# A two-layer transformer stack on one core: the second layer's first weight split is moved into the first layer's last steps

## The reference

```python
x = x + _layernorm(_L0_attn_ref(_layernorm(x), Wq, Wk, Wv, Wo))            # 32 heads, 8 key heads, rotary, causal
x = x + _layernorm(_L0_ffn_ref(_layernorm(x), lora_A, lora_B, W, bias, lora_weights))   # one 512x512 linear with LoRA
x = x + _layernorm(_L1_attn_ref(_layernorm(x), Wq, bq, Wk, bk, Wv, bv, Wo, bo, gq, gk)) # 32 heads, below
x = x + _layernorm(_L1_ffn_ref(_layernorm(x), w1, w3, w2, ...))                         # gated, 1376 wide

def _L1_attn_ref(hidden_states, Wq, bq, Wk, bk, Wv, bv, Wo, bo, gq, gk):
    q = rmsnorm((hidden_states @ Wq + bq).reshape(b, n, 32, 128), gq)
    k = rmsnorm((hidden_states @ Wk + bk).reshape(b, n, 32, 128), gk)
    v = (hidden_states @ Wv + bv).reshape(b, n, 32, 128)
    attn = softmax(einsum('bnhd,bmhd->bhnm', q, k) / sqrt(128))
    return einsum('bhnm,bmhd->bnhd', attn, v).reshape(b, n, 4096) @ Wo + bo
```

## Time and profile before

| | us |
|---|---|
| median of 3 runs | 2296.71 |
| profiled execution, its own time | 2295.63 |
| span of the profiled execution | 2293.8 |
| PE busy | 2107.2 (92%) |
| DVE busy | 1666.9 (73%) |
| ACT busy | 1350.7 (59%) |
| POOL busy | 1237.4 (54%) |

### The profile page before, as it was taken

How to read it: one execution, slowest core, us unless ns; L and a number is a source line. 1 busy time by engine, 2 the same in 40 slices (tenths; PEclk the granted TensorE clock), 3 DMA queues, 4 the chain that set the end, 5 groups by cost and what they waited for, 6 DMA issues and landing times. The chain is left out here.

```text
span 2293.8 us, 38455 instructions
## 1 busy us (share of the span) xinstructions
PE 2107.2 (92%) x10535; PEld 1778.1 (78%) x10535; DVE 1666.9 (73%) x2961; ACT 1350.7 (59%) x3637; POOL 1237.4 (54%) x996
## 2 busy tenths in 40 slices
PE   5899999999999747999999999999999999857998
PEld 4688888888887636888888888888888888636886
DVE  3788888888788743888778787887787888763322
ACT  4777777777776434666566665665656656433321
POOL 4878787787795533564454544545445454334400
PEclk8999999999999968999999999999999999977999
DMA  2344434434335220444444444434444443432210
GB/s 79 105 114 112 117 99 119 119 97 129 100 107 154 74 85 9 125 115 115 107 105 102 111 114 113 104 99 112 117 111 105 100 120 84 105 123 97 69 48 27
DMA packets 165903, 231.96 MB, mean 101 GB/s; under 512 B 47280, under 2 KB 77136, under 8 KB 165744
## 3 DMA queue, kind: packets, MB, share of 16 engines
q1 hardware_dynamic: 165744, 229.97, 37.7%
HBM read 114.23 MB, written 6.55 MB: 53 GB/s over the span
## 5 line engine op out<-in xcount | busy, mean ns | idle before, releaser
L90 POOL TENSOR_TENSOR l_probsT_lo<-l_moved,l_probsT_hi 128x512 fp32r<-128x512 f32 (+2 forms) x256 | 282.0, 1106 | 313.6 <-ACT l_probsT_hi L579 286.7
L573 ACT ACTIVATE l_probs<-l_score,l_negtop 128x512 f32<-128x512 f32 x256 | 175.7, 686 | 385.1 <-DVE l_negtop L675 384.7
L90 DVE TENSOR_TENSOR l_probsT_lo<-l_moved,l_probsT_hi 128x512 fp32r<-128x512 f32 (+1 forms) x256 | 285.9, 1117 | 30.5 <-ACT l_probsT_hi L579 30.5
L675 DVE TENSOR_REDUCE l_negtop<-l_score 128x1 f32<-128x512 f32 x256 | 175.7, 687 | 101.7 <-PE l_score L85 99.7
L1435 ACT ACTIVATE l_probs<-l_score,l_negtop 128x128 f32<-128x128 f32 (+3 forms) x256 | 134.8, 526 | 177.8 <-DVE l_negtop L1524 176.3
L83 PE MATMUL l_score<-l_kT_lo,l_qT_hi 128*128 128x512 f32 (+3 forms) x512 | 191.2, 373 | 50.4 <-POOL l_qT_lo L90 28.9
L83 PE MATMUL l_general<-l_w_qk_lo,xT_hi 128*128 128x512 f32 x512 | 201.6, 394 | 28.5 <-POOL l_w_qk_lo L90 28.5
L83 PE MATMUL l_out<-l_w_out_lo,l_oT_hi 128*128 128x512 f32 x512 | 209.3, 409 | 6.0 <-DVE l_oT_lo L90 3.2
L1524 DVE CUSTOM_DVE_ANT_0 l_score<-l_score,l_mask 128x128 f32<-128x128 f32 (+3 forms) x256 | 126.2, 493 | 113.1 <-PE l_score L85 112.0
L85 PE MATMUL l_out<-l_w_out_hi,l_oT_hi 128*128 128x512 f32 x512 | 201.6, 394 | 0.0
L84 PE MATMUL l_out<-l_w_out_hi,l_oT_lo 128*128 128x512 f32 x512 | 201.4, 393 | 0.0
(11 more groups left out here) (215 smaller groups left out, 6361.5 us busy)
## 6 DMA issues: line engine op xcount, KB each, us to landing
l_moved<-l_blocks SPq DMA_DIRECT2D x1024, 64.0 KB, 2.0
l_moved<-l_blocks SPq DMA_DIRECT2D x512, 80.0 KB, 2.1
l_inv_all<-inv_rows SPq DMA_DIRECT2D x32, 512.0 KB, 4.3
l_raw_out<-l_wo SPq DMA_DIRECT2D x64, 256.0 KB, 4.4
l_inv_all<-inv_rows SPq DMA_DIRECT2D x64, 256.0 KB, 3.6
ffn_w_lo_words<-f_w SPq DMA_DIRECT2D x33, 256.0 KB, 2.8
l_raw_q<-l_wq SPq DMA_DIRECT2D x32, 256.0 KB, 4.2
l_raw_qk<-l_wq SPq DMA_DIRECT2D x64, 128.0 KB, 2.9
```

Source lines behind the costliest of these rows:

```text
L90: return engine.tensor_tensor(out, full, hi.bitcast(F32), ALU.subtract)
L573: act.activation(probs[:, n % NPR], score[n % 2][:], ACT.Exp, bias=negtop[:, n:n + 1], accum_out=total[:, n:n + 1]).then_inc(s_exp, 1)
L675: dve.tensor_reduce(negtop[:, n:n + 1], score[n % 2][:], AXX, ALU.max, negate=True)\
```

## The change

A new class `Ahead` holds `raw_qk`, `w_qk`, `b_qk` and their semaphores, allocated before the first layer, in the first part of SBUF. The first layer's own tiles are laid over this part, and their order is changed so that what lies there (`moved` and `probsT_lo`, the raw weights and the lower weights) is no longer read when `Ahead` writes; `probs` and `blocks` move behind them.

In the last pass of the first layer SP loads the first pair's raw weights at step 51 (8 transfers, behind the last product with the probabilities, `pv` of slot 7) and its biases at step 59 (2 transfers). ACT makes the four upper parts at the ends of steps 59 to 62, POOL the four lower parts at the ends of steps 60 to 63. In the opening of the second layer these 10 transfers, 4 copies and 4 subtractions are gone. The second pair's raw weights and biases are now the first transfers, ahead of the constants. Its four upper parts follow on ACT behind the squares of the fourth `y` tile, and its four lower parts are made by DVE, no longer by POOL, behind the fourth `y` tile. The combination of the gains moves behind that tile too, and ACT waits for `s_zero` only where it uses the gains. Behind the opening the tables are as before.

```diff
+class Ahead:
+    LOAD, BIAS, SPLIT = 51, 59, 59
...
+    def load(self, sp):
+        for c in range(C):
+            for e in range(2):
+                sp.dma_start(self.raw_qk[:, 0, c, e * 2 * HD:(e + 1) * 2 * HD],
+                             self.a[("l1_wq", "l1_wk")[e]][c][:, 0:2 * HD]).then_inc(self.s_raw_qk[0], 16)
...
+    def upper(self, act, n):
+        c = n - self.SPLIT
+        if 0 <= c < C:
+            act.wait_ge(self.s_raw_qk[0], 2 * C * 16)
+            act.activation(self.w_qk.hi[:, 0, c], self.raw_qk[:, 0, c], ACT.Copy).then_inc(self.s_w_hi, 1)
+
+    def lower(self, pool, n):
+        c = n - self.SPLIT - 1
+        if 0 <= c < C:
+            pool.wait_ge(self.s_w_hi, c + 1)
+            rest(pool, self.w_qk.lo[:, 0, c], self.raw_qk[:, 0, c], self.w_qk.hi[:, 0, c]).then_inc(self.s_w, 1)
...
 # paired_attention, sync
-            fetch(start, FETCH1.early[0], 0)
-            for x in BIAS1.early:
+            for x in FETCH1.early[1:]:
+                fetch(start, x, 0)
+            for x in BIAS1.early[1:]:
                 bias(start, x[0], 0)
             sp.dma_start(gains[:, 0:1], a["l1_gq"]).then_inc(s_const, 16)
...
-            for x in FETCH1.early[1:]:
-                fetch(start, x, 0)
 # paired_attention, scalar
-            act.wait_ge(s_zero, 1)
-            for x in LOADS1.early[:C]:
-                work(x, start, 0)
-            for x in USES1.early:
+            for k, x in enumerate(USES1.early):
                 if of_halved(x):
+                    act.wait_ge(s_zero, 1)
                     bank_hi(x, start, 0)
                 else:
                     square(x, start, 0)
-            for x in LOADS1.early[C:]:
-                work(x, start, 0)
+                if k == TB - 1:
+                    for x in LOADS1.early[C:]:
+                        work(x, start, 0)
 # paired_attention, vector
-            dve.wait_ge(s_const, 64)
...
+                if k == TB - 1:
+                    dve.wait_ge(s_const, 64)
+                    dve.scalar_tensor_tensor(gains[:, 2:3], gains[:, 0:1], SCALE, gains[:, 1:2], ALU.mult, ALU.mult)\
+                        .then_inc(s_zero, 1)
+                    dve.wait_ge(s_zero, 1)
+                    for x in LOADS1.early[C:]:
+                        dve.wait_ge(s_w_hi, start.done(LOADS1, x))
+                        rest(dve, w_dest(x).lo, w_words(x), w_dest(x).hi).then_inc(s_w, 1)
 # paired_attention, gpsimd
-            for x in LOADS1.early[:C]:
-                work(x, start, 0)
             for x in USES1.early:
                 if x[0] == "y" and x[3] == TB - 1:
                     norm(x, start, 0)
-            for x in LOADS1.early[C:]:
-                work(x, start, 0)
 # grouped_attention: order of the tiles in SBUF
+        with ExitStack() as early:
+            moved = p.sb(early, "l0_moved", TRIANGLES)
+            raw_k, raw_v = p.sb(early, "l0_raw_k", [P, C * HD]), p.sb(early, "l0_raw_v", [P, C * HD])
+            raw_q, raw_out = p.sb(early, "l0_raw_q", [P, GH, C * HD]), p.sb(early, "l0_raw_out", [P, GH, D])
+        probsT_lo = sb("probsT_lo", TRIANGLES, F32R)
...
         probs = sb("probs", [P, NPR, S])
         blocks = sb("blocks", TRIANGLES)
 # grouped_attention, sync
+                    if m.last and n == Ahead.LOAD:
+                        sp.wait_ge(s_bank, m.done(USES0, ("pv", SLOTS - 1)))
+                        ahead.load(sp)
+                    if m.last and n == Ahead.BIAS:
+                        sp.wait_ge(s_out, TT + m.done(OUTS0, (SLOTS - 1, TB - 1)))
+                        ahead.load_bias(sp)
```

More of the change, by code:

```diff
@@ L291, in of_y, with __init__, load_bias, paired_attention @@
     return x[0] == "y"
-def paired_attention(p, ctx0, xT, acc, ident, half, inv_rows):
+class Ahead:
+    LOAD, BIAS, SPLIT = 51, 59, 59
+    WORDS = 2 * 2 * C * 512 + 2 * 512
+    def __init__(self, p, ctx0):
+        sem = lambda n: p.sem(ctx0, f"l1_{n}")
+        self.a = p.a
+        with ExitStack() as room:
+            with ExitStack() as early:
+                self.raw_qk = p.sb(early, "l1_raw_qk", [P, 2, C, 512])
+            lo = p.sb(room, "l1_w_qk_lo", [P, 2, C, 512], F32R)
+            self.w_qk = Split(p.sb(room, "l1_w_qk_hi", [P, 2, C, 512], F32R), lo)
+            self.b_qk = p.sb(room, "l1_b_qk", [P, 2, 512])
+        self.s_raw_qk, self.s_b = [sem("raw_qk0"), sem("raw_qk1")], [sem("b_qk0"), sem("b_qk1")]
+        self.s_w_hi, self.s_w = sem("w_hi"), sem("w")
+    def load(self, sp):
[3 more added lines that the diff above has]
+                             self.a[("l1_wq", "l1_wk")[e]][c][:, 0:2 * HD]).then_inc(self.s_raw_qk[0], 16)
+    def load_bias(self, sp):
+        for e in range(2):
+            rows = self.a[("l1_bq", "l1_bk")[e]][0:1, 0:2 * HD]
+            sp.dma_start(self.b_qk[:, 0, e * 2 * HD:(e + 1) * 2 * HD], rows.to_broadcast([P, 2 * HD]))\
+                .then_inc(self.s_b[0], 16)
+    def upper(self, act, n):
[8 more added lines that the diff above has]
+            rest(pool, self.w_qk.lo[:, 0, c], self.raw_qk[:, 0, c], self.w_qk.hi[:, 0, c]).then_inc(self.s_w, 1)
+def paired_attention(p, ctx0, xT, acc, ident, half, inv_rows, ahead):
     nc, a = p.nc, p.a
@@ L307, in paired_attention @@
         NPR, HW = 2, 2 * HD
+        sb("ahead", [P, Ahead.WORDS])
+        raw_qk, w_qk, b_qk = ahead.raw_qk, ahead.w_qk, ahead.b_qk
         probs = sb("probs", [P, NPR, S])
@@ L1065, in of_dve, with grouped_attention @@
     return x[0] in ("pv", "vt")
-def grouped_attention(p, ctx0, xT, acc, ident, half, x_rows, kept, inv_rows):
+def grouped_attention(p, ctx0, xT, acc, ident, half, x_rows, kept, inv_rows, ahead):
     nc, a = p.nc, p.a
@@ L1657, in body @@
                         linear.roots(pool, n)
+                        ahead.lower(pool, n)
             passes(pool, body, Linear.END)
@@ L2047, in _ @@
                 pool.wait_ge(made, 3)
-        grouped_attention(p, ctx, xT, acc, ident, half, x_rows, kept, inv_rows[0])
-        paired_attention(p, ctx, xT, acc, ident, half, inv_rows[1])
+        ahead = Ahead(p, ctx)
+        grouped_attention(p, ctx, xT, acc, ident, half, x_rows, kept, inv_rows[0], ahead)
+        paired_attention(p, ctx, xT, acc, ident, half, inv_rows[1], ahead)
         swiglu_phase(p, ctx, xT, xT_words, acc, ident, half, kept, out_rows)
```

22 lines of the change are left out of this document (8 added, 14 removed).

## The result

The changed kernel takes **2268.57 us** (median of 4 runs, 2266.79 to 2271.07), the kernel before 2297.74 (median of 4, 2292.23 to 2299.52): ratio 0.9878, 95% interval 0.9858 to 0.9898. That is 29.2 us less; 28.5 were forecast, and 2268. The profiled execution of the changed kernel is the slowest of its four: 2271.07 us, span 2269.3 at a clock of 0.965.

What follows compares the result with a forecast made beforehand. PE fills the second layer's passes, so its waits before them count in full. -17.4 - 9.4 - 2.2 + 0.5 = -28.5 us from the profiled 2295.63 gives 2267.1; 2268 us from the median, range 2263.5 to 2276.

Steps and rivals of the forecast that it cites:

- First wait: Layer boundary: with the first pair's lower parts ready, PE starts near 841.1 instead of 858.49, gaining 17.4 us.
- Second wait: Score tile 1 of the second layer: PE no longer waits for POOL's lower parts of the second pair, gaining 9.4 us.
- the clock behind it: The `y` tile at step 1: its 12 matmuls follow warm work, 2.73 instead of 4.90 us, gaining 2.2 us.
- POOL, +0.5: Second layer's opening: DVE's subtractions beside POOL's root lengthen the norm PE waits for, costing 0.5 us (bounds 0 and 0.55).
- The port held by the root: Rival: POOL's root holds the shared SBUF port, DVE's subtractions wait, first score tile some 2 us late; 2270 us, chance 0.13.
- DVE's delay, 0: Opening: the four subtractions keep DVE from the fifth `y` tile for some 2.3 us, costing nothing.
- The first layer's last steps: Added transfers, copies and subtractions cost 0 of 0 to 7.3 us; rival that they grow: 2275 us, chance 0.08.
- Second wait moves: Rival: PE still stands at step 1 or 4, so only the first 17.4 us are gained; 2279 us, chance 0.07.
- addresses: First layer's moved tiles cost 0; rival that new addresses collide and slow its 256 score tiles: 2304 us, chance 0.03.
- late load: Rival: a late load holds ACT at its first copy in the first layer's last steps; time about unchanged, chance 0.01.
- the cases in which it is faster by over 7 us: All cases but the slower one (addresses) and the late load; chance given as 0.95, the forecast itself having 0.68.

Runs made afterwards that it cites:

- the changed kernel's second profile: The changed kernel run again unaltered, on another chip than its first profile; 2267.53 us, ratio 0.9886 to the kernel before.
- the second part alone: The kernel before, with only the second pair split behind the fourth `y` tile, upper parts by ACT, lower by DVE; 2281.44 us, ratio 0.9944.
- the last version: The changed kernel with the last `y` tile ahead of q's transposition and the copies of q and k ahead of its squares; 2264.89 us, again 2260.26.
- The layout alone: The kernel before with only the new tile addresses, nothing loaded or split ahead, opening in its old order; 2293.46 us, ratio 0.9995.
- third profile of the changed kernel: The changed kernel unaltered once more, on the chip of the last version's second run; 2265.04 us, ratio 0.9871 to the kernel before.
- the later split: The changed kernel with the first pair's split five steps later in the first layer's last steps; 2270.54 us, ratio 0.9897 to the kernel before.
- either part alone: The kernel before with only the first pair loaded and split ahead (2275.82 us), or only the second pair's split moved (2281.44 us).
- POOL between the norms: The changed kernel with the second pair's lower parts made by POOL between its two norms instead of by DVE; 2264.92 us, ratio 0.9875.
- the split over the multiplications: The changed kernel with DVE's four subtractions two `y` tiles later, over POOL's four norm multiplications instead of its root; 2268.31 us.

## Why the prediction was right, and where it was not

- **First wait, -17.4.** Right: 17.75 to 0.33 us, and 0.32 to 0.34 in every profile in which the first pair is ahead. The start stood at 0.50 of the clock, as said.
- **Second wait, -9.4, and the clock behind it, -2.2.** Right as a mechanism. In the changed kernel's second profile, and with the second part alone, it came to 11.66 and 11.65 us for 11.6. In the profile that goes with the result it was 20.93 - 11.93 = 9.0: the step that failed there is "without the wait the 12 matmuls of that tile follow warm work". They followed, two cold score tiles later, a 3.07 us wait which the sum had taken for harmless, since the kernel before kept its clock in it. It is not: in two of three profiles of the changed kernel the clock fell in it, at 2.7 us a time. The forecast of 2.7 us for that tile held in one profile of three (3.79 in the first).
- **POOL, +0.5.** The term was wrong, and its reading too. POOL's root of batch 0 stayed at 2.91 us under DVE's four subtractions. The 3.46 us in the earlier trace rows were put down to DVE's seven copies; where k is subtracted before the root and only the copies run beside it, as in the last version, the root takes 3.01. So most of the 0.55 us goes with DVE's subtraction of k, which lay beside the root wherever it took 3.46. The term should have been 0.
- **The port held by the root.** The rival did not come: the four subtractions took 2.50 us together, 0.62 each, beside the root. The doubt "the trace agrees for the subtractions and not for the root" was the right one. But it was nearly right about the danger: moved by two tiles, the same four instructions met the multiplications and cost 2.7 to 2.9 us up to score tile 0, the fall of the clock included. As it stands they end at 859.34 and the multiplications begin at 859.49.
- **DVE's delay, 0.** DVE took the fifth and sixth `y` tile one behind the other from 859.25, and PE's waits ahead of score tile 0 stayed at 1.41 and 3.07 us, as before.
- **The first layer's last steps, 0 of 0 to 7.3.** Right by the gaps named, shown by 25.92 against 25.88 us; five steps later it would have been 2.2.
- **Second wait moves; addresses; late load.** None came. The layout alone was 0.05% below the kernel before, too little to tell from nothing, and the raw weights were issued by 784.1 us, 24 us ahead of the first copy at 808.50.
- **The sum.** 28.5 forecast, 29.2 by the medians, 27.4 and 26.2 in the repeats on other chips (by the ratios 28.0, 26.2 and 29.6). The ruler, which the passes don't blur, has 26.4, 29.3 and 26.4. That the forecast came out at 0.6 us from the median owes something to luck, since the missing 0.5 at POOL and the clock's occasional 2.7 pull opposite ways, and executions of one kernel lie several us apart. The chances of the cases in which it is faster by over 7 us add up to 0.96, where the text has 0.95.

## What to carry to other kernels

Work that one engine makes for another at the head of a phase goes into the idle gaps of the phase before, and the gap must be read at the very step: the same eight instructions cost 0 us beside a 5 us gap and 2.2 us five steps later. When a long wait is removed, look at the short waits ahead of it as well; they may decide at which clock the freed stretch runs. Before a DVE instruction with two SBUF operands is moved, look at which of GpSimd's instructions it will lie beside, since 2.50 us there can be 5.22 a little later. And where the runs spread over more than the effect, marks within one execution are the better ruler, for the stretch between them.

## What the runs showed of the hardware that was not expected

- The same wait of 3.07 to 3.08 us for k's lower part, after the same work, dropped PE's granted clock to 0.50 in some executions (the first and third profile of the changed kernel, the later split, the split over the norm) and not in others (the kernel before, the second profile of the changed kernel, either part alone, the layout alone, POOL between the norms). One program did both, so the order of its instructions does not decide it; what does stays open. The clock dropped right behind the wait of 2.74 us, in the split over the multiplications, as well; waits of 1.6 to 1.7 us in three profiles did not drop it, and the one of 9.4 us did each time. After a drop, the stretch from score tile 0 to 4 took 10.5 to 12.0 us in place of 9.2 to 9.3.
- GpSimd's root (128x16 elements, 2.91 us) and DVE's subtractions of two SBUF operands (128x512) did not slow each other at all, while GpSimd's multiplications (128x512) and the same subtractions slowed to 5.38 and 5.22 us from 4.04 and 2.50. GpSimd's instructions are thus not alike in this; whether the operation or its size makes the difference was not tested. The Trainium skill, SBUF — State Buffer, SBUF: two separate sides, has an instruction hold the port throughout; beside the root the runs do not show it, and the measurement decides.
